# Graph attention and mixture-of-experts kernel: gather order, attention's argument, TensorE's first stage, and a third tile in plain fp32

## The reference

```python
def gnn(input, adj, W, a1, a2):
    h = input @ W
    e = leaky_relu(h @ a1 + (h @ a2).T, negative_slope=0.2)
    attention = softmax(where(adj > 0, e, -9e15), axis=1)
    return relu(attention @ h)

def ffn(x, Wr, br, W1, b1, W2, b2):
    probs = softmax(x @ Wr + br)
    gate, idx = max(probs), argmax(probs)
    mask = one_hot(idx, E)
    pos = (cumsum(mask, axis=0) * mask).astype(int32)     # a row is dropped from position C on
    mask = mask * (pos < C)
    combine = gate * mask * one_hot(idx) x one_hot(pos, C)
    expert_in = einsum('nd,nec->ecd', x, combine)
    h = relu(einsum('ecd,edf->ecf', expert_in, W1) + b1)
    eo = einsum('ecf,efd->ecd', h, W2) + b2
    return einsum('ecd,nec->nd', eo, combine)

x = x + gnn(layernorm(x), adj, W, a1, a2)
x = x + ffn(layernorm(x)[None], Wr, br, W1, b1, W2, b2)[0]
```

## Time and profile before

| | us |
|---|---|
| median of three runs | 282.66 |
| the three runs | 281.39, 282.66, 284.98 |
| the profiled execution | 283.06 |
| its span, first to last instruction | 281.3 |
| TensorE busy | 261.1 |
| VectorE, ScalarE, GpSimd busy | 150.4, 110.5, 74.7 |

### The profile page before, as it was taken

The page is one execution under the profiler, slowest core; times in us unless marked ns, Lnnn a source line. Parts: engine busy times, 40 slices in busy tenths (PEclk is TensorE's granted clock), DMA queues, the critical chain, the costliest instruction groups (busy, mean ns, idle before and its releaser), DMA issues.

```text
span 281.3 us, 4639 instructions
## 1 busy us (share of the span) xinstructions
PE 261.1 (93%) x1688; PEld 230.8 (82%) x1688; DVE 150.4 (53%) x386; ACT 110.5 (39%) x228; POOL 74.7 (27%) x107
## 2 busy tenths in 40 slices
PE   5999989999989999999999999989399999999990
PEld 1479989988868888888888778789399999999980
DVE  3948958996766865875753647621312232232031
ACT  2265785855456455555542301121212222222110
POOL 5224770000122012012022051247051441421122
PEclk9999999999998999999999999999989999999997
DMA  7970000331387868321120112119957789784001
GB/s 231 341 262 15 1 3 0 101 99 21 125 254 234 267 209 240 135 82 67 45 77 37 39 56 78 38 49 280 282 142 234 237 242 275 221 261 151 11 7 41
DMA packets 18201, 38.62 MB, mean 137 GB/s; under 512 B 2698, under 2 KB 3018, under 8 KB 18180
## 3 DMA queue, kind: packets, MB, share of 16 engines
q1 hardware_dynamic: 15188, 32.34, 36.5%
q0 software_dynamic: 2176, 4.80, 6.1%
q10 hardware_dynamic: 816, 1.21, 1.2%
HBM read 31.10 MB, written 8.31 MB: 140 GB/s over the span
## 4 chain that ended last, share of the span: by engine, by line
PE 75%; issue 5%; DVE 5%; DMA 4%; POOL 4%; ACT 4%; POOLq 0%; DVEq 0%; SPq 0%; ACTq 0%
PE bank L1254 26%; PE bank L1445 22%; PE bank L1192 5%; PE bank L1240 4%; PE bank L1275 3%; DMA vecs<-x_rows,src 3%; PE bank L1174 3%; PE bank L1475 2%; PE bank L1264 2%; PE bank L1437 1%; PE bank L1144 1%; DVE adj_s L809 1%; POOL wide L412 1%; DMA vecs<-in_L_gnn_a_dram 1%; PE bank L1161 1%
## 5 line engine op out<-in xcount | busy, mean ns | idle before, releaser
L1254 PE MATMUL bank<-h_hi,pt_lo 128*128 128x512 f32 (+3 forms) x121 | 51.0, 421 | 0.0
L1254 PE MATMUL bank<-h_lo,pt_hi 128*128 128x512 f32 (+3 forms) x121 | 48.5, 401 | 0.0
L1254 PE MATMUL bank<-h_hi,pt_hi 128*128 128x512 f32 (+3 forms) x121 | 48.4, 400 | 0.0
L1445 PE MATMUL bank<-adj_s,w 128*128 128x168 f32 x256 | 39.4, 313 | 0.9 <-ACT adj_s L659 0.9
L1445 PEld LDWEIGHTS bank<-adj_s,w 128*128 128x128 f32 x256 | 38.1, 196 | 1.3 <-issue 1.3
L1445 PE MATMUL bank<-prob,w 128*128 128x168 f32 x256 | 38.3, 306 | 0.4 <-ACT prob L649 0.4
L1445 PEld LDWEIGHTS bank<-prob,w 128*128 128x128 f32 x256 | 36.9, 190 | 1.1 <-issue 1.1
L381 POOL TENSOR_TENSOR x_all<-x_all,w_raw 128x512 f32<-128x512 f32 x10 | 12.7, 1273 | 63.5 <-ACT w_raw L557 63.5
L1254 PEld LDWEIGHTS bank<-h_hi,pt_hi 128*128 128x128 f32 (+3 forms) x121 | 22.7, 187 | 6.1
L659 ACT ACTIVATE adj_s<-bank,b_cols 128x168 f32<-128x168 f32 x32 | 11.0, 398 | 42.0 <-PE bank L1445 37.6
L1254 PEld LDWEIGHTS bank<-h_hi,pt_lo 128*128 128x128 f32 (+3 forms) x121 | 22.6, 187 | 4.6
(11 more groups left out here) (153 smaller groups left out, 433.7 us busy)
## 6 DMA issues: line engine op xcount, KB each, us to landing
w<-in_L_ffn_W_dram SPq DMA_DIRECT2D x16, 1024.0 KB, 6.9
adj_s<-in_adj_dram SPq DMA_DIRECT2D x10, 677.0 KB, 4.0
x_rows<-x_all SPq DMA_DIRECT2D x10, 257.0 KB, 3.7
out_dram<-x_all SPq DMA_DIRECT2D x10, 256.0 KB
x_all<-in_x_dram SPq DMA_DIRECT2D x9, 256.0 KB, 4.2
w_raw<-in_L_gnn_W_dram ACTq DMA_DIRECT2D x4, 256.0 KB, 4.4
adj_s<-in_adj_dram SPq DMA_DIRECT2D x1, 391.4 KB
x_all<-x_rows,src POOLq DMA_INDIRECT x10, 6.8
```

The costliest lines, as they stand in the source:

```text
L1254: ins = pe.matmul(o_ps[par][0:R, :], p[0:K, par, k, 0:R], h[0:K, k, :], start=(k == 0 and n == 0), stop=(k == NT - 1 and n == 2))
L1445: ins = pe.matmul(ps[f // 2][:, (f % 2) * CAP:(f % 2 + 1) * CAP], w[:, c, f * P:(f + 1) * P], v[:, c, :], start=(c == 0), stop=(c == KC - 1))
```

## The change

Seven edits in hand-written order, two of which take instructions away or put other ones in their place. Expert 2's gather is issued right behind expert 1's, ahead of expert 0's second one, and SyncE waits for it before it loads expert weights. VectorE runs `argument(t + 2)` ahead of `p_low(t + 1, ., 0)`. TensorE's `logits(0)` is moved behind the next product of attention. At the start, the six spins between `spread_a` and the first transposition are gone, four more stand in the first row of spins, and the spread of a2 comes behind the transposition of tile 0. Tile 2's product takes W in plain fp32, as those of tiles 0 and 1 do, so `x_low(2)` is gone, and ScalarE's `normal(2)` and `bias_rows` change places with their neighbours.

```diff
+    PLAIN = 3
@@ sync
-            sp.wait_ge(s_x1g[1], 32)
+            sp.wait_ge(s_x1g[2], 32)
             sweep(sp, load_expert, 0, 0, E, start=2)
@@ gpsimd
             gather_x1(1)
+            gather_x1(2)
             pool.wait_ge(s_x1g[1], 32)
             pool.wait_ge(s_xg, 2)
             gather_x1(0)
             pool.wait_ge(s_dest, 1)
-            for e in range(2, E + 2):
+            for e in range(3, E + 2):
@@ scalar
-                if t < 2:
+                if t < PLAIN:
+                    if t >= 2:
+                        act.wait_ge(s_h, t - 1)
                     act.activation(x2t[:, par, :, 0:R], src_[:, :, 0:R], ACT.Copy).then_inc(s_xhi, 1)
@@
-            w_high(1)
             normal(2)
+            w_high(1)
             normal(3)
...
-            bias_rows()
             normal(4)
             x_high(4)
             h_high(2)
+            bias_rows()
@@ vector
-            x_low(2)
@@
                 p_low(t, par, 2)
-                p_low(t + 1, 1 - par, 0)
                 if t + 2 < NT:
                     argument(t + 2)
+                p_low(t + 1, 1 - par, 0)
@@ tensor
-            spin(4)
+            spin(8)
@@ h_raw
                 pe.wait_ge(s_xhi, t + 1)
+                after(pe, s_hlo, t, 2)
...
-                    ins = pe.matmul(h_ps[t][j][:, 0:c1 - c0], x2t[:, t, c, :], w_raw[:, c, c0:c1],
+                    ins = pe.matmul(h_ps[t % 2][j][:, 0:c1 - c0], x2t[:, t % 2, c, :], w_raw[:, c, c0:c1],
@@
-            spread_a()
-            spin(6)
+            spread_a(0)
             x_turn(0)
+            spread_a(1)
             h_raw(0, 0)
...
             x_turn(3)
-            for t in range(2, NT - 4):
+            h_raw(2, 0)
+            h_raw(2, 1)
+            x_turn(4)
+            for t in range(PLAIN, NT - 4):
@@
                 attend(t, par, 0)
-                logits(t - 2, par)
+                if t > 2:
+                    logits(t - 2, par)
                 p_turn(t + 1, 1 - par, 1)
                 attend(t, par, 1)
+                if t == 2:
+                    logits(0, 0)
```

More of the change, by code:

```diff
@@ L462, in x_high @@
                 src_ = xt_ps[par][:, :].rearrange("p (c n) -> p c n", c=KC)
-                if t < 2:
+                if t < PLAIN:
+                    if t >= 2:
+                        act.wait_ge(s_h, t - 1)
                     act.activation(x2t[:, par, :, 0:R], src_[:, :, 0:R], ACT.Copy).then_inc(s_xhi, 1)
                 else:
-                    if t >= 4:
+                    if t >= PLAIN + 2:
                         act.wait_ge(s_h, t - 1)
@@ L500, in bias_rows @@
                 act.wait_ge(s_wlo, 2)
-                act.wait_ge(s_h, 2)
+                act.wait_ge(s_h, PLAIN)
                 act.dma_start(b_rows[:, 0, :], b1.rearrange("e (c p) -> (e c) p", p=P)).then_inc(s_bias, 16)
@@ L515, in _ @@
             x_high(1)
+            normal(2)
             w_high(1)
-            normal(2)
             normal(3)
@@ L1135, in spin, with spread_a @@
                               start=True, stop=True)
-            spin(4)
+            spin(8)
             pe.wait_ge(s_const, 3)
-            def spread_a():
-                for i in range(2):
-                    pe.wait_ge(s_a[i], 16)
-                    pe.matmul(row_ps[i][:, :], half[0:1, :].broadcast_to([1, P]), a_rows[:, i, :], start=True,
-                              stop=True).then_inc(s_ab, 1)
+            def spread_a(i):
+                pe.wait_ge(s_a[i], 16)
+                pe.matmul(row_ps[i][:, :], half[0:1, :].broadcast_to([1, P]), a_rows[:, i, :], start=True,
+                          stop=True).then_inc(s_ab, 1)
             def x_turn(t):
@@ L1152, in x_turn @@
                     pe.wait_ge(s_xn, t)
-                if t >= 4:
-                    pe.wait_ge(s_xlo, t - 3)
+                if t >= PLAIN + 2:
+                    pe.wait_ge(s_xlo, t - PLAIN - 1)
                 elif t >= 2:
@@ L1187, in h_half @@
                     elif n == 1:
-                        pe.wait_ge(s_xlo, t - 1)
+                        pe.wait_ge(s_xlo, t - PLAIN + 1)
                     else:
@@ L1213, in f2_turn @@
                 pe.wait_ge(s_wa2b, 1)
-                pe.wait_ge(s_xlo, 6)
+                pe.wait_ge(s_xlo, 8 - PLAIN)
                 for b in range(3):
@@ L1229, in p_turn @@
                     pe.wait_ge(s_f2b, 3)
-                    pe.wait_ge(s_xlo, NT - 3)
+                    pe.wait_ge(s_xlo, NT - 1 - PLAIN)
                 elif t == 1:
@@ L1379, in _ @@
             pe.wait_ge(s_bias, 32)
-            pe.wait_ge(s_xlo, NT - 2)
+            pe.wait_ge(s_xlo, NT - PLAIN)
             for j in range(2):
```

## The result

The changed kernel took 273.53 us, the median of four runs (271.16 to 276.37), beside a median of 282.71 of the kernel before on the same chip. The ratio is 0.964, with a 95% interval of 0.9542 to 0.9738: faster. It is estimated from the executions in the chip's faster state alone (276.37 is left out), so it is not the quotient of the two medians, which is 0.968. The profiled execution took 273.54 us, with a span of 271.8, where the one before had 283.06 and 281.3. The forecast was 273.0.

The account below looks back on a forecast made before the run. TensorE's own work was taken to bound the kernel nearly everywhere. Gains of 5.8 (gathers), 2.8 (attention) and 1.4 (start) sum to 10.0 us off the profiled 283.06, giving 273.1, stated as 273.0; range 270.0 to 276.5.

Parts of the forecast that it names:

- Part 1: Experts: earlier gather of expert 2 and SyncE's wait remove TensorE's 4.38 us idle and a slow layer; gain 5.8 us.
- I take 3.3, because SyncE now holds the weights back: Expert 2's last gather transfer takes 3.3 us, not 8.1, since it meets quiet engines while weights wait.
- The rival of the late gather: Experts: expert 2's rows still take 8.1 us, or weights come late; gather edits worth 1.1; 277.7 us, chance 0.04.
- Part 2: Attention: the 1.32 us wait at the first logits and 1.52 us of low clock behind it go; gain 2.8 us.
- gains nothing beyond the 2.8: Attention, VectorE: argument ahead of p_low costs nothing and adds nothing, its low part being wanted one tile later.
- is covered by 1.9 us: Attention: with logits(0) behind the next twelve products, TensorE's wait for ScalarE's copy is covered by 1.9 us.
- the rival in which the clock falls all the same: Attention: narrow matmuls and transpositions, not the gap, lower the clock; 274.5 us, chance 0.09.
- Part 3: Start: new spin and spread order brings first products earlier, less 0.7 for tile 2's plain product; gain 1.4 us.
- the near ends: Start: tile 1's first half product at 12.7 or 14.8 us, so a gain of 2.4 or 0.4.
- The cold start: Start: first products run at 1.2 GHz, gain from 0.4 down to -1.5; 275.0 us, chance 0.17.
- The price of the third plain tile: Start: tile 2's plain product takes 3.73 us where high and low parts took 3.00; costs 0.7 us.
- The rival in which the first products all stay at half clock: Start: plain products stay at 1.2 GHz, six half products cost 1.87 us more each; 283.3 us, chance 0.02.

Follow-up runs that it names:

- without the hold: Changed kernel with SyncE waiting only for expert 1's rows before loading weights, the gathers in their new order; 273.0 us, ratio 0.9619 to the kernel before.
- the gap filled: Kernel before with seven spins in TensorE's gap ahead of logits(0), which keeps its old place; 284.29 us, ratio 0.9999.
- gathers alone: Kernel before with expert 2's gather right behind expert 1's and SyncE waiting for it; 279.67 us, ratio 0.9803.
- start alone: Kernel before with only the start's edits: spins, spread of a2, third tile plain, ScalarE's two orders; 279.67 us, ratio 0.9845.
- hold alone: Kernel before with only SyncE's new wait, holding expert weights until expert 2's rows land, gathers in old order; 276.07 us, ratio 0.9717.
- four spins: Changed kernel with four spins, not eight, ahead of the spread of a1; 274.38 us, ratio 0.9707 to the kernel before.
- two plain tiles: Changed kernel with tile 2's product in high and low parts again; 271.17 us, 0.9541, then 272.41 us, 0.9612, to the kernel before.

## Why the prediction was right

**The whole.** 273.0 forecast, 273.53 measured, and 9.5 us between the profiled executions where the sum had 10.0. The three errors are +0.01, +0.34 and -0.88, and partly cancel. That the number came within 0.5 us is luck in part: ten executions of the changed kernel took 271.16 to 276.76 us.

**Part 1, right in size and in each time.** The last issue was put 3.9 us behind the first (3.91; 183.92 and 3.9 are 187.8, not the 187.9 of the text), and the transfer at 3.3 us (3.2). What is late next was put at the end of ScalarE's relu, 0.8 us behind the end of the first layer, with the transposition in between; the relu ends 0.7 behind it, and the second layer starts 0.8 behind it. The stretch fell from 22.44 to 16.63. The load of weights wanted first landed 6.8 us after 187.68, so at 194.5, where it is wanted at 199.96. One step was too narrow. "I take 3.3, because SyncE now holds the weights back" names the hold as the condition. The runs show two sufficient causes: to be issued ahead of the weights, or to have them held. The rival of the late gather had it take 8.1 us although the weights are held; it took 3.2, and without the hold TensorE does not wait for it either.

**Part 2, right in size, with a wrong step and one that is half luck.** The wrong step is that the argument "gains nothing beyond the 2.8" since its low part has ten microseconds to spare. That looked at who waits for the low part, not at who waits for what stood behind it: VectorE's offsets, ScalarE's `low_slope`, and in the same stream the very copy that TensorE wanted. The logits' move alone would have left a wait of 0.58 one tile on, and the claim that the wait "is covered by 1.9 us" held for tile 0 only. Both halves together take 1.59, where I counted 1.32; where the other 0.27 comes from is open.

The rest of the 3.14, some 1.55, is the low clock, which I counted as part of what the gap costs. In the trace of before it did. But of four traces with that gap only two show the fall. So part 2 is worth 1.6 in one execution and 3.1 in another, and the rival in which the clock falls all the same named a cause that the runs don't bear out: no kernel without the gap shows a fall in attention, in seven traces, and neither do the three with a gap of 0.6 us or with the gap filled, though the narrow matmuls and transpositions are in all of them. The page "TensorE: Matmul & The Clock Gate" of the Trainium skill, section "Why this matters for your kernels", which asks only that one avoid idle gaps much longer than 1.3 us, was weighed against this. Two traces here (before and gathers alone, 0.50 behind the gap) go against it and two (start alone and hold alone, 1.00) agree, so neither it nor my reading is the whole rule. The larger gap, of 3.5 to 4.4 us in front of expert 2's transposition, was followed by a fall in all six traces that have it, and in none of the eight without it.

**Part 3, a mis-sized term.** The start gave 0.52 in the profiled execution where the term was 1.4, the middle of 0.4 and 2.4. The working of the near ends was good: tile 1's product was to start at 12.7 or 14.8, and it did so at 14.86 in one trace and at 12.60 in the other. What I took for an unknown of one kernel is a spread between executions of the same kernel. It is read best at tile 4's transposition, since from there to x1 of tile 0 all fourteen traces take 49.88 to 49.98 us:

| start of the first stage | tile 4's transposition starts at |
|---|---|
| old (seven traces) | 25.89, 25.92; 28.17, 28.23, 28.37, 28.47, 28.64 |
| new (seven traces; 25.20 has four spins) | 22.62, 22.87, 22.92, 23.15; 25.20, 25.40; 26.26 |

The trace of before that the sum was made against has one of the two early old starts, and the changed kernel's first trace one of the late new ones, so the difference came out small. By the means of the table, 27.67 and 24.06, it is 3.6 us, and the kernel with part 3 alone is 4.4 us faster (0.9845, so 2.4 to 6.4). The times of the whole change say less: 9.2 us between the medians, less 5.8 for the gathers and 1.6 to 3.1 for attention, leave 0.3 to 1.8. What the new start is worth over many executions stays open; 1.4 is between these figures, but the table shows that the term had no single value. The cold start was seen as well: 26.26 is 0.34 behind the old start of the profile, within its -1.5. The price of the third plain tile, put at 0.7, is 0.15 to 0.46. The rival in which the first products all stay at half clock did not come: beside the first half product, the most that a trace shows is 5.79 us in place of 3.73 for the two half products behind it, in the kernel without the hold.

## What to carry to other kernels

A stall on a secondary engine is worth what stands behind it in its own stream, and then what stands behind that on the next engine: follow the stream to the instruction on which the bounding engine waits before writing that a move gains nothing. A small transfer wants to be issued ahead of bulk loads, or the bulk held until it has landed; either one is enough, so look which costs less. And where the clock's rise differs between executions of one kernel, take the duration of a known instruction in several traces before any start-up term is sized from one.

## What the runs showed of the hardware

**The clock's rise at the start is not set by the kernel alone.** The granted clock of the seven traces with the old start is at its upper level from 11.5 or 11.6 us in two and from 17.0 to 18.1 in five, with the same instructions; tile 4's transposition differs by 2.25 to 2.75 us between the groups. With eight spins in one row the clock was up between 4.2 and 5.7 us in five traces of six, but in four of the five it fell again at 7.6 to 9.1 us, under the spread of a2 and the first half product, and came back at 11.9 to 12.5 (three) or at 17.9. It stayed up in one.

**The clock column of a window can mislead at the start.** For 6 to 8 us it reads 1.00 in the kernel before too (TensorE alone), though the spread of a1 and a2 takes 3.75 us there for four instructions:

```profile
6.00:8.00 2.00, 2.00 (x4) 1.00 0.95 293
```

Two instructions of that spread take 2.04 in the changed kernel's first trace and 1.09 to 1.12 where the clock is up throughout. The durations tell the level, the column does not, as long as no change of the clock has been recorded.

**Plain fp32 is not much dearer than high and low parts here.** By TensorE's starts a tile's product takes 3.47 us in plain fp32 (19.68 to 23.15, the changed kernel's second trace) and 2.98 in three products (19.94 to 22.92, two plain tiles).
